# Weighing the values of four heads in one item, in the causal stage of a four-stage kernel

## The chip, the core and the metric

The kernel runs on one core of a Trainium2 chip. The metric is the device time of one execution in microseconds (us). Engines: PE (TensorE, matrix products into PSUM), DVE (VectorE), ACT (ScalarE), POOL (GpSimd), SP (which issues the DMAs here).

## The reference, cut to what matters

Four layers follow each other on x of shape (4, 1024, 128): attention over a window of 64, a gated linear attention, a causal attention mixed with a fast-weight recurrence, and a mixture of experts. The change is in the third:

```python
q, k, v = split(layernorm(x) @ Wqkv_w + Wqkv_b)        # 16 heads of 8 columns
scores = einsum('bhid,bhjd->bhij', q, k) * scale
attn = softmax(scores + causal_mask)                   # 1024 x 1024 per head, masked above the diagonal
y_softmax = einsum('bhij,bhjd->bhid', attn, v)
# y_stp: y_t = (W_static + state_t) q_t, state_t = retention * state + Gamma * v_t k_t^T
y = alpha * y_softmax + (1 - alpha) * y_stp            # alpha: a gate, per token and head
x = x + y @ out_w + out_b
```

## The kernel before, in words

The four stages run one after the other: window, gla, causal, moe. In the trace the causal stage's first scores are at 1058 us and its last weighing ends at 1750.

In the causal stage a unit is a batch b and a group g of four heads; there are 16. Queries are rows in chunks of 512 columns (c = 0, 1), keys are in blocks of 128 rows (j). A key step is a pair (c, j) that the mask doesn't empty: 4 for c = 0 and 8 for c = 1, 12 per unit. Its queries are those of chunk c from block j on. In a unit that is six steps of 512 columns, two of 384, two of 256 and two of 128.

PE works through one list of items, `order`, in that order, and the other engines go through the same list for their part of each item:

- M (lines 1092 to 1112): scores with queries on the partitions, for the row maxima. DVE reduces them (line 1261). 20 per unit, each of up to 2 x 512 columns. They belong to the unit after the one whose W and V surround them.
- S (1113): the negative maxima turned, after POOL has split them in three (1513 to 1519); ACT copies them (1365) and SP's DMAs put them into the stack as three more rows.
- W (1120 to 1138): scores with keys on the partitions, two heads (half i of the group) on two halves of the array's rows, bf16, then on a diagonal block two mask products (1133, 1136). ACT takes the exponential (1375) into one of four buffers `c_probs`.
- V (1139 to 1158): the weighing. For each of two heads an fp32 product of 128 key rows by 9 columns (8 values and a one, whose sum is the softmax's denominator) into partitions 32h of the accumulator `acc`, summed over j.
- A (1376): ACT copies a finished chunk's accumulator to `c_o_T`.

Beside them run the next batch's norm and projections (turn, q, k, v, gate1, gate2, vT), the finish of the previous batch (att, tp), and the recurrence: for each of 8 columns a product on POOL (kv, 1526), a scan on DVE (1271), a scale on ACT (1388) and two passes on POOL (read, 1538 and 1541), two columns per unit.

M, S, W, att, tp and the projections take turns in three PSUM slots of two banks, `ring`. Before PE writes an item it waits until the item three places earlier in the ring has been read (`pe_wait_free`, 1010). V doesn't use the ring: it goes to `acc`, of which there are two, one per chunk in turn.

The list is made by `causal_order` (855). It holds prices of each item for PE, ACT and DVE (`TIMES`, `times`), keeps a clock for each, and puts row scores M ahead of a W or V as long as they are at least 9 and at most 19 key scores ahead of need; between these bounds it does so where the item would begin no later than the W or V and DVE isn't behind ACT (`put_ahead`, 960). Each W is followed by the V of three W before:

Of the kernel before, what the change touches and what calls it, by code (L numbers as in the profile page):

```python
# [13 lines left out]
P = 128  # L14
BANK = 512
EPS = 1e-5
HEADS, HD = 16, 8
GROUP = 4
GROUPS = HEADS // GROUP
# [97 lines left out]
def build(nc, x_in, packed, x_out, place, batches, T, known):  # L117
# [7 lines left out]
    with ctx:  # L125
# [36 lines left out]
        acc = [accs[:, i * BANK:(i + 1) * BANK] for i in range(2)]  # L162
# [692 lines left out]
        def causal_order():  # L855
# [55 lines left out]
            def times(item):  # L911
# [4 lines left out]
                if item[0] in "WV":  # L916
                    c, j = item[3:5]
                    a = max(c * BANK, j * P)
                    cols = (c + 1) * BANK - a
                    if item[0] == "V":  # L920
                        return 0.02 + 0.00103 * cols, (), 0
                    return 0.00077 * cols + (0.15 if a == j * P else 0), (("A", 0.17 + 0.00166 * cols),), 1
# [6 lines left out]
            def begin(item):  # L929
                t = clock["P"]  # L930
                if times(item)[2]:
                    t = max(t, free[0])
                return max(t, made[item[1:]]) if item[0] == "V" else t

# [35 lines left out]
            for u in units:  # L970
                for k, (c, j) in enumerate(KEY_STEPS):
                    for i in range(2):
# [3 lines left out]
                        while sums:  # L976
                            put(sums.pop())
                        late.append(("V", *u, c, j, i))
                        if len(late) > 3:
                            item = late.pop(0)  # L980
                            put_ahead(item)
                            put(item)
                            if item[4:] == ((item[3] + 1) * BANK // P - 1, 1):
                                sums.append(("A", *item[1:4]))
                    for item in side[(u[0] * GROUPS + u[1]) * len(KEY_STEPS) + k]:
# [4 lines left out]
        def causal():  # L990
# [49 lines left out]
            def pe_program():  # L1040
# [3 lines left out]
                for item in order:  # L1044
# [94 lines left out]
                    elif kind == "V":  # L1139
                        _, b, g, c, j, i = item  # L1140
                        a = first_query(c, j)
# [4 lines left out]
                        pe.wait_ge(c_cleared, ("ones", 1))  # L1146
                        if j == 0 and i == 0 and ci >= 2:
                            pe.wait_ge(c_copied, ci - 2)
                        pe.wait_ge(c_weights_made, ("W", *item[1:]))
                        weights = c_probs[w_index["W", b, g, c, j, i] % 4]  # L1150
                        for r in range(2):
                            h = 2 * i + r
                            mm = nc.tensor.matmul(  # L1153
                                acc[ci % 2][32 * h:32 * h + HD + 1, a - c * BANK:BANK],
                                c_values[b % 2][:, j, r * HEADS // 2 + 2 * g + i, :],
                                weights[:, r * BANK:r * BANK + (c + 1) * BANK - a],
                                start=j == 0, stop=j == (c + 1) * BANK // P - 1, skip_group_check=True)
                        mm.then_inc(c_weighed.up(item), 1)
# [26 lines left out]
            def dve_program():  # L1185
# [10 lines left out]
                for item in order:  # L1196
# [42 lines left out]
                    elif kind == "v":  # L1239
                        _, b, h = item  # L1240
                        dv.wait_ge(c_valued, (b, h))
                        if b >= 2:
                            dv.wait_ge(c_weighed, ("V", b - 2, GROUPS - 1, *KEY_STEPS[-1], 1))
                        nc.vector.tensor_tensor(
# [57 lines left out]
            def act_program():  # L1302
# [5 lines left out]
                for item in order:  # L1308
# [58 lines left out]
                    elif kind == "W":  # L1367
# [5 lines left out]
                        if wi >= 4:  # L1373
                            ac.wait_ge(c_weighed, ("V", *w_items[wi - 4][1:]))
                        nc.scalar.activation(view(c_probs[wi % 4]), view(ps), ACT.Exp).then_inc(c_weights_made.up(item), 1)  # L1375
                    elif kind == "A":
                        _, b, g, c = item
                        ac.wait_ge(c_weighed, ("V", b, g, c, (c + 1) * BANK // P - 1, 1))
                        if b:
# [1244 lines left out]
```

## Time and profile before

| | |
|---|---|
| Time, median of 3 runs | 2084.08 us (2080.84 to 2087.06) |
| The profiled execution | 2081.97 us, its span 2080.6 us |
| PE busy | 1812.6 us, 87% |
| DVE busy | 1295.3 us, 62% |
| ACT busy | 1134.7 us, 55% |
| POOL busy | 660.3 us, 32% |

Busy time is that of instructions; the end of a matmul is modelled and holds the time its last results need to leave the array, which overlaps the next item. A record of a matmul starts where its columns start to stream, so the time an item takes on PE is best read from its start to the start of the next. An fp32 matmul leaves two records, a bf16 one leaves one.

### The profile page before, as it was taken

The numbers are of one execution on the slowest core, as the hardware profiler recorded it, in microseconds if no ns is written. First come the engines' busy times: TensorE is split into PE (matmuls) and PEld (weight loads), VectorE is DVE, ScalarE is ACT, GpSimd is POOL, SyncE is SP. The second block draws the span as 40 slices with busy tenths as digits, with TensorE's granted clock in tenths as the row PEclk, the third lists the DMA queues.
The fourth block names the chain that finished last, engine by engine and source line by source line (L and its number), as shares of the span: only waits on it lengthen the run. The fifth ranks groups of instructions, "written<-read, shape, count | busy, mean of one in ns | idle before, by whom it ended". The sixth has DMA issues, their size and how long they took to land.

```text
span 2080.6 us, 45291 instructions
## 1 busy us (share of the span) xinstructions
PE 1812.6 (87%) x19452; PEld 1056.7 (51%) x19472; DVE 1295.3 (62%) x2096; ACT 1134.7 (55%) x1720; POOL 660.3 (32%) x468
## 2 busy tenths in 40 slices
PE   4688879999999999999658899799889988598799
PEld 2456646776677677677522324233333423355465
DVE  5566536666666666666566776586677663555544
ACT  2365647667666766766315676566566665222221
POOL 5220004342343434235504442544444344000000
PEclk8899969999999999999858999899999999799999
DMA  6754000000000000000161532252262220000000
GB/s 166 215 132 96 7 9 1 2 1 1 2 2 1 1 2 2 1 2 2 73 148 42 161 77 50 88 137 63 82 143 62 62 63 21 0 11 6 6 11 11
DMA packets 38361, 102.08 MB, mean 49 GB/s; under 512 B 3856, under 2 KB 12176, under 8 KB 34704
## 3 DMA queue, kind: packets, MB, share of 16 engines
q1 hardware_dynamic: 38160, 99.18, 18.5%
q8 instruction: 153, 2.51, 0.5%
q14 instruction: 48, 0.39, 0.1%
HBM read 66.93 MB, written 31.46 MB: 47 GB/s over the span
## 4 chain that ended last, share of the span: by engine, by line
PE 56%; DVE 20%; issue 8%; ACT 5%; POOL 4%; DMA 1%; POOLq 0%; DVEq 0%; SPq 0%; ACTq 0%
PE accs L1153 8%; DVE arena L1261 4%; PE ring L1870 3%; PE accs L1934 3%; PE ring L2364 3%; PE ring L2366 3%; PE accs L2333 3%; PE ring L1896 3%; PE ring L1129 2%; PE ring L1103 2%; DVE arena L1271 2%; PE ring L1864 2%; PE ring L1835 2%; DVE arena L2023 1%; DVE arena L2063 1%
## 5 line engine op out<-in xcount | busy, mean ns | idle before, releaser
L1261 DVE TENSOR_REDUCE arena<-ring 128x2 f32<-128x1024 f32 (+2 forms) x320 | 346.1, 1112 | 148.1 <-PE ring L1110 97.2
L1375 ACT ACTIVATE arena<-ring 128x1024 f32<-128x1024 f32 (+3 forms) x384 | 304.3, 808 | 174.4 <-PE ring L1136 139.0
L1153 PE MATMUL accs<-arena 128*9 128x512 f32 (+3 forms) x1536 | 322.2, 500 | 0.0
L1129 PE MATMUL ring<-arena 51*128 51x512 bf16 (+3 forms) x768 | 133.5, 342 | 26.7 <-DVE arena L1261 14.8
L1103 PE MATMUL ring<-arena 48*128 48x512 bf16 (+3 forms) x768 | 131.5, 353 | 22.7 <-DVE arena L1261 10.0
L2248 POOL TENSOR_TENSOR arena<-arena 128x1280 f32<-128x1280 f32 x28 | 65.3, 2332 | 265.2 <-PE accs L1934 234.6
L1129 PEld LDWEIGHTS ring<-arena 51*128 51x128 bf16 x768 | 37.9, 94 | 207.0 <-issue 82.9
L2240 POOL TENSOR_TENSOR arena<-arena 128x512 f32<-128x512 f32 x112 | 138.9, 1272 | 10.2 <-DVE arena L2044 10.2
L2232 POOL TENSOR_TENSOR arena<-arena 128x1024 f32<-128x1024 f32 x32 | 75.6, 2364 | 190.2 <-DVE arena L2063 190.2
L2443 DVE TENSOR_TENSOR arena<-arena,ring 128x512 f32<-128x512 f32 x80 | 55.0, 688 | 122.7 <-PE ring L2366 112.2
L2493 ACT ACTIVATE arena<-ring 128x512 f32<-128x512 f32 x80 | 47.8, 597 | 147.0 <-PE ring L2364 147.0
L1538 POOL TENSOR_TENSOR arena<-arena 128x1024 f32<-128x1024 f32 x28 | 65.9, 2352 | 190.5 <-ACT arena L1388 147.9
L294 PE MATMUL ring<-weights_constants,xn 128*128 128x128 f32 x124 | 35.4, 379 | 84.1 <-DVE xn L278 52.6
L1271 DVE TENSOR_TENSOR_SCAN arena<-arena 128x1024 f32<-128x1024 f32 x32 | 79.5, 2484 | 34.5 <-POOL arena L1526 34.5
L2333 PEld LDWEIGHTS accs<-weights_large,arena 128*128 128x128 f32 x640 | 85.1, 193 | 29.2 <-issue 26.3
L2063 DVE TENSOR_TENSOR arena<-ring,arena 128x1024 f32<-128x1024 f32 x32 | 39.2, 1225 | 85.9 <-PE ring L1896 85.9
L1896 PE MATMUL ring<-arena 64*128 64x128 f32 x1024 | 91.7, 285 | 0.2
L1896 PEld LDWEIGHTS ring<-arena 64*128 64x128 f32 x1024 | 79.2, 187 | 19.5 <-issue 12.9
L2159 ACT ACTIVATE arena<-ring 128x1024 f32<-128x1024 f32 x32 | 32.8, 1024 | 100.7 <-PE ring L1835 100.7
L1996 DVE SCALAR_TENSOR_TENSOR arena<-ring,arena 128x1024 f32<-128x1024 f32 x32 | 39.2, 1225 | 76.0 <-ACT arena L2163 76.0
L1103 PEld LDWEIGHTS ring<-arena 48*128 48x128 bf16 x768 | 38.3, 97 | 94.9 <-issue 34.8
L2333 PE MATMUL accs<-weights_large,arena 128*128 128x128 f32 x640 | 85.0, 276 | 1.5 <-DVE arena L2449 0.5
(334 smaller groups left out, 4365.5 us busy)
## 6 DMA issues: line engine op xcount, KB each, us to landing
arena<-whole_k SPq DMA_DIRECT2D x32, 512.0 KB, 4.6
arena<-whole_q SPq DMA_DIRECT2D x32, 512.0 KB, 6.2
arena<-a_scratch_q SPq DMA_DIRECT2D x16, 384.0 KB, 6.9
arena<-a_scratch_k SPq DMA_DIRECT2D x16, 384.0 KB, 8.3
arena<-c_scratch_q SPq DMA_DIRECT2D x16, 384.0 KB, 8.2
arena<-c_scratch_k SPq DMA_DIRECT2D x16, 384.0 KB, 10.1
a_scratch_k<-arena SPq DMA_DIRECT2D x8, 512.0 KB, 3.9
c_scratch_k<-arena SPq DMA_DIRECT2D x8, 512.0 KB, 5.2
```

The costliest lines, as they stand in the source:

```text
L1103: mm = nc.tensor.matmul(o[r], qs[half(r, SCORE), pair, n * P:(n + 1) * P], ks[half(r, SCORE), pair, a:c], start=True, stop=not diag)
L1129: mm = nc.tensor.matmul(ps[:, r * BANK:r * BANK + cols], ks[half(r, SHIFT), pair, j * P:(j + 1) * P], qs[half(r, SHIFT), pair, a:a + cols] ...
L1153: mm = nc.tensor.matmul(acc[ci % 2][32 * h:32 * h + HD + 1, a - c * BANK:BANK], c_values[b % 2][:, j, r * HEADS // 2 + 2 * g + i, :], weig ...
L1261: nc.vector.tensor_reduce(dst, src, AX.X, ALU.max, negate=True).then_inc(c_max_taken.up(item), 1)
L1271: nc.vector.tensor_tensor_scan(sk[:, :], c_retain[:, j:j + 1].to_broadcast([P, T]), sk[:, :], 0.0, ALU.mult, ALU.add).then_inc(c_state_mad ...
L1375: nc.scalar.activation(view(c_probs[wi % 4]), view(ps), ACT.Exp).then_inc(c_weights_made.up(item), 1)
L1538: nc.gpsimd.tensor_tensor(sq[:, :], sk[:, :], sq[:, :], ALU.mult).then_inc(c_y_step.up((b, j)), 1)
L1896: mm = nc.tensor.matmul(ps[:, r * BANK + p * P:r * BANK + (p + 1) * P], k_[t % 2][half(r), p * P:(p + 1) * P], q_[t % 2][half(r), p * P:(p ...
L2232: nc.gpsimd.tensor_tensor(masked[0][:, :], masked[0][:, :], masked[1][:, :], ALU.add).then_inc(gla_joined.up(t), 1)
L2240: nc.gpsimd.tensor_tensor(pair_cols(q2m[t % 2][:, r, :]), pair_cols(q2[t % 2][:, :]), hot_b[:, r * P:(r + 1) * P].unsqueeze(1).to_broadcas ...
L2248: nc.gpsimd.tensor_tensor(state_mid[:, :, :, :].rearrange("p a r d -> p (a r) d"), state[:, :, :, :].rearrange("p a r d -> p (a r) d"), fa ...
L2333: mm = nc.tensor.matmul(total[:, n * P:(n + 1) * P], hid[index[item] % 3][:, n * P:(n + 1) * P], w("d_down", f * P, (f + 1) * P), start=f ...
```

## The change

V becomes an item of a key step, not of a half step: it weighs all four heads of the group with four matmuls in a row, from two `c_probs` buffers, and raises its semaphore once. The order becomes W(k, 0), W(k, 1), V(k−1): the weighing of a step comes behind both scores of the next. It waits for the second exponential of its step. What waited for V(…, 1) now waits for V of the step, and the exponential of W number wi waits for the V of the step in which W number wi − 4 was. The planner prices a V at 0.00205 us per column (four heads) where it was 0.02 + 0.00103 per column (two heads), and has one place for row scores ahead of a V per step. The scores and their masks, 128 columns wide, are as they were.

```diff
                     if item[0] == "V":
-                        return 0.02 + 0.00103 * cols, (), 0
+                        return 0.00205 * cols, (), 0
...
-                return max(t, made[item[1:]]) if item[0] == "V" else t
+                return max(t, made[item[1:] + (1,)]) if item[0] == "V" else t
...
                         while sums:
                             put(sums.pop())
-                        late.append(("V", *u, c, j, i))
-                        if len(late) > 3:
-                            item = late.pop(0)
-                            put_ahead(item)
-                            put(item)
-                            if item[4:] == ((item[3] + 1) * BANK // P - 1, 1):
-                                sums.append(("A", *item[1:4]))
+
+                    late.append(("V", *u, c, j))
+                    if len(late) > 1:
+                        item = late.pop(0)
+                        put_ahead(item)
+                        put(item)
+                        if item[4] == (item[3] + 1) * BANK // P - 1:
+                            sums.append(("A", *item[1:4]))
...
-                        _, b, g, c, j, i = item
+                        _, b, g, c, j = item
...
-                        if j == 0 and i == 0 and ci >= 2:
+                        if j == 0 and ci >= 2:
                             pe.wait_ge(c_copied, ci - 2)
-                        pe.wait_ge(c_weights_made, ("W", *item[1:]))
-                        weights = c_probs[w_index["W", b, g, c, j, i] % 4]
-                        for r in range(2):
-                            h = 2 * i + r
-                            mm = nc.tensor.matmul(
...
+                        pe.wait_ge(c_weights_made, ("W", *item[1:], 1))
+                        for i in range(2):
+                            weights = c_probs[w_index["W", b, g, c, j, i] % 4]
+                            for r in range(2):
+                                h = 2 * i + r
+                                mm = nc.tensor.matmul(
+                                    acc[ci % 2][32 * h:32 * h + HD + 1, a - c * BANK:BANK],
+                                    c_values[b % 2][:, j, r * HEADS // 2 + 2 * g + i, :],
+                                    weights[:, r * BANK:r * BANK + (c + 1) * BANK - a],
+                                    start=j == 0, stop=j == (c + 1) * BANK // P - 1, skip_group_check=True)
                         mm.then_inc(c_weighed.up(item), 1)
...
                         if wi >= 4:
-                            ac.wait_ge(c_weighed, ("V", *w_items[wi - 4][1:]))
+                            ac.wait_ge(c_weighed, ("V", *w_items[wi - 4][1:5]))
```

## Rows read from the trace of the kernel before

**Rows 1.** The page, part 4: the chain that ended last, by engine.

```profile
PE 56%; DVE 20%; issue 8%; ACT 5%; POOL 4%; DMA 1%; POOLq 0%; DVEq 0%; SPq 0%; ACTq 0%
```

**Rows 2.** Stretches: length, busy us of PE, PEld, DVE, ACT, POOL; granted clock; DMA.

```profile
0.00:600.00 600.00, 498.60 (x8113) 351.17 (x8114) 362.66 (x690) 353.76 (x579) 178.27 (x152) 0.93 0.21 55
1060.00:1089.00 29.00, 17.66 (x146) 7.17 (x142) 25.73 (x27) 1.01 (x1) 3.32 (x5) 0.50 0.37 78
1089.00:1750.00 661.00, 604.29 (x5484) 213.72 (x5486) 441.63 (x468) 413.57 (x523) 287.78 (x196) 0.95 0.33 84
1192.00:1262.00 70.00, 67.23 (x668) 21.80 (x666) 54.65 (x47) 47.14 (x59) 32.02 (x22) 1.00 0.31 76
1306.00:1367.00 61.00, 50.89 (x414) 18.74 (x416) 39.25 (x37) 33.82 (x41) 29.03 (x20) 0.89 0.50 137
1437.00:1481.00 44.00, 40.48 (x374) 17.99 (x372) 27.16 (x52) 26.57 (x37) 17.39 (x15) 0.99 0.20 50
1688.00:1723.00 35.00, 31.66 (x264) 8.72 (x260) 15.79 (x13) 23.34 (x29) 16.58 (x11) 0.90 0.26 62
1723.00:1750.00 27.00, 26.54 (x220) 7.38 (x218) 5.41 (x2) 22.05 (x29) 14.71 (x8) 1.00 0.16 40
```

**Rows 3.** Groups by line and shape: line 1153, busy us and mean ns.

```profile
L1153 PE MATMUL accs<-arena 128*9 128x512 f32 x768 | 204.2, 610 | 0.0
...
L1153 PE MATMUL accs<-arena 128*9 128x384 f32 x256 | 52.5, 488 | 0.0
...
L1153 PE MATMUL accs<-arena 128*9 128x256 f32 x256 | 39.5, 392 | 0.0
...
L1153 PE MATMUL accs<-arena 128*9 128x128 f32 x256 | 26.3, 288 | 0.0
```

**Rows 4.** Order of time: start us, length us, engine, line, what, count.

```profile
1209.36 0.39 PE L1129 MATMUL ring<-arena 51*128 51x512 bf16 x2
...
1209.59 0.38 PE L1103 MATMUL ring<-arena 48*128 48x512 bf16 x2
1209.80 1.02 ACT L1375 ACTIVATE arena<-ring 128x1024 f32<-128x1024 f32 x1 [0.37 <-PE ring L1129]
...
1209.90 1.03 PE L1153 MATMUL accs<-arena 128*9 128x512 f32 x4
...
1210.87 0.39 PE L1129 MATMUL ring<-arena 51*128 51x512 bf16 x2
...
1211.19 1.03 PE L1153 MATMUL accs<-arena 128*9 128x512 f32 x4
...
1214.26 0.38 PE L1103 MATMUL ring<-arena 48*128 48x512 bf16 x2
...
1214.57 1.03 PE L1153 MATMUL accs<-arena 128*9 128x512 f32 x4
1214.68 1.23 DVE L1261 TENSOR_REDUCE arena<-ring 128x2 f32<-128x1024 f32 x1 [0.21 <-PE ring L1103]
```

**Rows 5.** Order of time, PE, end of the stage.

```profile
1748.62 0.82 PE L1153 MATMUL accs<-arena 128*9 128x384 f32 x4
...
1749.61 0.94 PE L1153 MATMUL accs<-arena 128*9 128x256 f32 x16
1750.49 0.33 PE L1164 MATMUL ring<-weights_constants,arena 128*128 128x128 f32 x1
```

**Rows 6.** Line 1153 alone in two stretches of 0.05 us (x: matmul records).

```profile
1748.60:1748.65 0.05, 0.04 (x2) 1.00 0.00 0
1749.60:1749.65 0.05, 0.04 (x4) 1.00 0.00 0
```

**Rows 7.** Groups of DVE, 1100 to 1750 us.

```profile
L1261 DVE TENSOR_REDUCE arena<-ring 128x2 f32<-128x1024 f32 x173 | 206.9, 1220 | 63.9 <-PE ring L1103 47.2 <-PE ring L1110 15.4
L1271 DVE TENSOR_TENSOR_SCAN arena<-arena 128x1024 f32<-128x1024 f32 x32 | 79.5, 2484 | 34.5 <-POOL arena L1526 34.5
```

**Rows 8.** Group of line 1117, the sum S, with PE's idle time before it.

```profile
L1117 PE MATMUL ring<-ident,arena 128*12 128x128 bf16 x128 | 10.6, 230 | 12.1 <-POOL arena L1519 7.8 <-ACT arena L1332 4.2
```

More of the change, by code:

```diff
@@ L1146, in pe_program @@
                         pe.wait_ge(c_cleared, ("ones", 1))
-                        if j == 0 and i == 0 and ci >= 2:
+                        if j == 0 and ci >= 2:
                             pe.wait_ge(c_copied, ci - 2)
-                        pe.wait_ge(c_weights_made, ("W", *item[1:]))
-                        weights = c_probs[w_index["W", b, g, c, j, i] % 4]
-                        for r in range(2):
-                            h = 2 * i + r
-                            mm = nc.tensor.matmul(
[L1154 to L1157, printed above, removed]
+                        pe.wait_ge(c_weights_made, ("W", *item[1:], 1))
[8 more added lines that the diff above has]
+                                    start=j == 0, stop=j == (c + 1) * BANK // P - 1, skip_group_check=True)
                         mm.then_inc(c_weighed.up(item), 1)
@@ L1242, in dve_program @@
                         if b >= 2:
-                            dv.wait_ge(c_weighed, ("V", b - 2, GROUPS - 1, *KEY_STEPS[-1], 1))
+                            dv.wait_ge(c_weighed, ("V", b - 2, GROUPS - 1, *KEY_STEPS[-1]))
                         nc.vector.tensor_tensor(
@@ L1377, in act_program @@
                         _, b, g, c = item
-                        ac.wait_ge(c_weighed, ("V", b, g, c, (c + 1) * BANK // P - 1, 1))
+                        ac.wait_ge(c_weighed, ("V", b, g, c, (c + 1) * BANK // P - 1))
                         if b:
```

## The prediction

> **What bounds the kernel now.** Read first the page's chain of waits [rows 1]: more than half of the span hangs on PE, and the reader should ask in which stage that is. The stretches of the causal stage [rows 2] answer it. The stage proper runs from 1089 to 1750 us: PE is busy 604.3 of 661 us (91%), DVE 441.6 (67%), ACT 413.6 (63%). In the quiet stretch 1192:1262 (two units of 12 key steps, with no projections) PE is busy 67.2 of 70 us. There PE sets the pace. In 1306:1367, where the next batch is projected, PE is busy only 50.9 of 61 us: the rest is waiting for other engines' links in a chain.
>
> Next, what PE does there. Line 1153, the weighing, has 1536 matmul records, two for each fp32 matmul, four for a V item [rows 3]: 204.2 + 52.5 + 39.5 + 26.3 = 322.5 us, over half of PE's time in the stage. In the order of time [rows 4], a V over 512 columns starts at 1209.90, the next W at 1210.87: 0.97 us on PE's path, since the last 0.06 of its 1.03 overlap. W to M takes 0.23 us, W to V 0.32, M to V 0.31: going over to the weighing costs about 0.09.
>
> **Part 1: four heads in one item.** Half i writes PSUM partitions 64i to 64i+31 and 64i+32 to 64i+63, so the four matmuls of a step lie in four different column strips. Do they stream together? Before, a W always parts the two halves, except at the very end, where four V items stand in a row. There 16 records over 256 and 128 columns take from 1749.61 to 1750.49 = 0.88 us [rows 5]. Inside 0.05 us four of them start, where a lone V starts two [rows 6]. Two at a time would be two V of 256 columns (39.5 / 64 − 0.07 = 0.55 each) and two of 128 (26.3 / 64 − 0.07 = 0.34): 1.78 us. Four at a time is 0.55 + 0.34 = 0.89. So four heads cost PE what two did: 0.97 us at 512 columns instead of 1.93.
>
> PE's path loses half of (322.5 − 384 × 0.07) = 148 us, and 192 of 384 crossings to the weighing at 0.09 = 17 us: 165 us of work. The same fp32 products are made, with the same weights and moving tiles; 384 increments of a semaphore become 192; no DMA moves, and nothing passes a wait of SP's or POOL's queue.
>
> **Part 2: the weighing stands behind both W of the next step.** V waits for the second exponential of its own step, two W back instead of three. With one M between them the ring's slot for the second W has already made PE wait for that exponential, so 0. ACT's exponential of W(k+1, 0) waits for V(k−1), which stands before it on PE: V is over 1.03 us after its start, the W is issued at 0.97 and read 0.44 later (1209.36 to 1209.80), so 0. Behind that wait on ACT stand the copies A and S and the scale; they wait no longer than before. A comes once per chunk as before. Cover gone, either wait would cost at most an exponential's 1.02 us; 0 to 0.4 us in few of 192 steps is what the rows allow, and I take 0.
>
> **Part 3: the planner.** Its price for weighing a full step goes from 2 × (0.02 + 0.00103 × 512) = 1.09 to 1.05 us, practically the same. It was 1.8 times too cheap for what it described and is now about right. Row scores keep their lead of 9 to 19 key scores; there are three places per step to put one instead of four, and two will often stand close together.
>
> **Where the 165 us go.** Four ring items per step (2 W, about 1.75 M or S) share three slots. A slot comes back after W's 0.44 + 1.02 + some 0.05 = 1.5 us, or after M's 0.42 + 1.23 + 0.05 = 1.7 (M at 1214.26, DVE from 1214.68). Now a full step is 2 × (0.23 + 0.31 + 0.97) = 3.02 us of pure PE, and slots are back in time since each V of 0.97 covers the return. After, PE would need 4 × 0.23 + 0.09 + 0.97 = 1.98. But the first ring item behind a V must be back before the fourth goes, and only then comes the next V: 1.5 to 1.7, + 0.31, + 0.97 = 2.78 to 2.98. DVE's two reductions are 2.46. A step with one M is bound by ACT's two exponentials, 2.04, plus hops: 2.1. With 0.75 of the steps of the first kind: 0.75 × 2.88 + 0.25 × 2.1 = 2.69, against 0.75 × 3.02 + 0.25 × 2.79 = 2.96 now. That is 0.27 us × 6 full steps = 1.6 us per unit. The 384-column steps drop from 2.7 to some 2.5; the two 256 and two 128 steps are held by DVE (2.46 for two reductions) and give 0 to 0.4 each. Sum: 1.6 + 0.4 + 0.8 = 2.8 us per unit at least, since these chains take the worst order each time. The upper side: the most loaded engine sets a quiet unit, DVE with 54.7 / 2 = 27.3 of 35 us, so 7.7 saved. I take 4, nearer to the chains, because three slots leave DVE no queue.
>
> By stretches [rows 2]: 7 quiet units × 4 = 28. Four units with the attention's finish (1437:1481: PE 40.5 of 44, DVE 27.2, ACT 26.6, few row scores), PE down to about 30: 5 each, bounds 2 and 10, = 20. Three units with the projections, 61 us, a third of PE's saving lost in waits that stay: 4 each = 12, bounds 0 and 10. 1688:1723 has few row scores; 2.57 us a step falls to ACT's 2.1: 6. The last, 1723:1750, is pure PE (26.5 of 27) and becomes ACT's, 22.1 busy: 4. Together 70. Against it: the sum S, for which PE waited 12.1 us [rows 8] on POOL and ACT, comes sooner, and the two scans per unit (2.48 us on DVE [rows 7]) have less cover: both lie inside "4, not 7.7". The clock takes 4 (below). Net 66: 2082 (this execution: span 2080.6, 1.4 around it) becomes 2016; the median shown, 2084, is 2 higher, and I forecast **2017 us**.
>
> The clock [rows 2]: in 1060:1089, where PE only feeds DVE's reductions (17.7 of 29 us busy), the granted clock is 0.50, the lower level, 1.2 GHz. In 0:600 PE is busy 83% and the clock 0.93; in 1192:1262 it is 1.00. After, PE would be busy some 75 to 80% in quiet units, in small pieces; by the rows 0:600 that costs a few hundredths, 4 us in my sum. The Trainium skill (TensorE: Matmul & The Clock Gate, "A second HAM failure mode: psum-queue depth-cycling") warns of just this shape, frequent short idles between groups that wait for PSUM, and of a clock that swings. By that rule the gain shrinks or turns; it is rival D. The trace speaks only half for it: 0:600 waits so too and stays high.
>
> **Rivals.** A (70%): the above, 1975 to 2055.
> B (12%): slots bind less than I say; the most loaded engine sets each unit. 7 × 7.7 + 4 × 10 + 3 × 9 + 8 + 4.5 = 133 saved: 1950. For it: DVE and ACT have a third of idle time. Against: the three slots.
> C (9%): the 1.3 us block of V starves DVE and ACT each step and what PE saves is all given back; 2075 to 2090. For it: 2.98 against 3.02 in the worst order. Against: steps without row scores must gain.
> D (6%), slower: with PE idle in small pieces the clock falls in the stage as in 1060:1089. At 1.2 GHz a full step is PE 4 × 0.45 + 0.1 + 1.93 = 3.8 us against 3.02. It eats the gain (0.3 a full step) from about a quarter of the stage at the low level; at half of it the time is 2110.
> E (3%), the change doesn't do what it says: four matmuls don't stream together. The Trainium skill (same page, "The mechanism") says that weights load beside running matmuls only where row groups differ, and these all use the same 128 rows. The four starts within 0.05 us speak against it. Then V is 1.93 in one block, only 17 us of crossings go, and the ring starves longer: 2095.
>
> **How the numbers follow.** The likeliest is A: 2017. The range 1960 to 2075 takes in half of B and the edge of C. Less than 0.3% (6 us, what a measurement of this kernel can tell from no change) is most of C; D, E and a little of C are slower: faster 0.86, same 0.07, slower 0.07.
>
> **What would show it.** Four records of line 1153's shape starting together, its busy sum near 165 us; PE's idle in 1192:1262's successor from 3 to over 12 us per pair of units, released by lines 1261 and 1375; DVE's share in quiet units from 78% to 85 or 90; 512-column steps at 2.6 to 2.9 us; the last unit near 23 us and set by ACT. Wrong if line 1153 keeps 322 us (E), if the granted clock of the stage falls below 0.88 (D), or if PE idle grows by as much as its work falls (C).

## The result, and the profile after

The changed kernel takes 2048.62 us (median of 6, 2044.53 to 2056.35), the kernel before 2083.48 (median of 6 in all): a ratio of 0.9835, 95% interval 0.9813 to 0.9857. It is faster by 35 us, 1.7%. The forecast was 2017 (1960 to 2075): the time lies in the range, the gain is about half of the 66 us that were forecast. The profiled execution is 2048.85 us, its span 2047.5.

The page: busy time by engine, and the chain that ended last by engine, against [rows 1].

```profile
PE 1710.9 (84%) x19472; PEld 1046.7 (51%) x19472; DVE 1288.2 (63%) x2096; ACT 1127.3 (55%) x1720; POOL 658.5 (32%) x468
...
PE 52%; DVE 24%; issue 7%; ACT 5%; POOL 4%; DMA 1%; POOLq 0%; DVEq 0%; SPq 0%
```

The stretches of the causal stage (length, busy us of PE, PEld, DVE, ACT and POOL, granted clock, DMA), against [rows 2]. The first is the stage, then two quiet units, a unit with projections, one with the attention's finish, another with projections, and the last two units.

```profile
1094.00:1717.00 623.00, 498.20 (x5478) 203.47 (x5478) 434.65 (x467) 405.45 (x523) 285.63 (x196) 0.88 0.35 88
1193.00:1256.00 63.00, 52.44 (x676) 20.74 (x673) 51.88 (x46) 46.41 (x60) 30.52 (x21) 0.96 0.37 87
1297.00:1363.00 66.00, 50.20 (x414) 19.58 (x412) 39.75 (x37) 33.47 (x40) 30.35 (x21) 0.73 0.49 132
1427.00:1469.00 42.00, 34.77 (x380) 17.43 (x376) 28.46 (x53) 26.11 (x38) 18.42 (x15) 0.90 0.21 52
1469.00:1531.00 62.00, 45.69 (x414) 18.65 (x414) 39.02 (x36) 33.50 (x41) 30.37 (x21) 0.80 0.49 135
1664.00:1692.00 28.00, 22.14 (x257) 7.39 (x256) 13.54 (x11) 21.93 (x30) 12.98 (x10) 0.85 0.30 77
1692.00:1717.00 25.00, 19.80 (x206) 5.79 (x204) 5.41 (x2) 21.10 (x29) 14.56 (x8) 0.86 0.18 43
```

The stage went from 661 us to 623. PE is busy 498.2 us in it, 105 less; it idles 125 us, 68 more. DVE and ACT have the work they had. The granted clock of the stage fell from 0.95 to 0.88: by the trace TensorE is at the lower level, 1.2 GHz, for 152 us of the stage, before for 63. In the projection units shown it is 0.73 and 0.80.

The weighing by shape (line 1155 is 1153 of before), against [rows 3], and the matmul records of that line in 0.05 us, against [rows 6]:

```profile
L1155 PE MATMUL accs<-arena 128*9 128x512 f32 x768 | 113.9, 669 | 2.2 <-ACT arena L1377 2.2
...
L1155 PE MATMUL accs<-arena 128*9 128x384 f32 x256 | 26.8, 491 | 0.6 <-ACT arena L1377 0.6
...
L1155 PE MATMUL accs<-arena 128*9 128x256 f32 x256 | 22.8, 433 | 0.0
...
L1155 PE MATMUL accs<-arena 128*9 128x128 f32 x256 | 14.8, 305 | 0.9 <-ACT arena L1377 0.9
```

```profile
1206.84:1206.89 0.05, 0.04 (x4) 1.00 0.00 0
```

The sum is 178.3 us, 144 less than the 322.5 of before, and in this V four records start within 0.05 us. The scores' matmuls, W and M on the page, before and then after:

```profile
L1129 PE MATMUL ring<-arena 51*128 51x512 bf16 (+3 forms) x768 | 133.5, 342 | 26.7 <-DVE arena L1261 14.8
L1103 PE MATMUL ring<-arena 48*128 48x512 bf16 (+3 forms) x768 | 131.5, 353 | 22.7 <-DVE arena L1261 10.0
```

```profile
L1130 PE MATMUL ring<-arena 51*128 51x512 bf16 (+3 forms) x768 | 133.5, 360 | 63.2 <-DVE arena L1263 48.8
L1104 PE MATMUL ring<-arena 48*128 48x512 bf16 (+3 forms) x768 | 140.0, 372 | 54.1 <-DVE arena L1263 14.7
```

Why is PE's busy time only 105 us lower, when the weighing's is 144 lower? All other matmuls of the stage together grew from 335 to 343 us. The rest is overlap: the weighing's records overlapped those of their neighbours for 53 us before and for 23 after, since there are half as many seams.

Three steps in the order of time, against [rows 4]:

```profile
1206.31 0.39 PE L1130 MATMUL ring<-arena 51*128 51x512 bf16 x2 [0.66 <-DVE arena L1263]
...
1206.54 0.38 PE L1104 MATMUL ring<-arena 48*128 48x512 bf16 x2
...
1206.85 1.04 PE L1155 MATMUL accs<-arena 128*9 128x512 f32 x8
...
1207.83 0.61 PE L1130 MATMUL ring<-arena 51*128 51x512 bf16 x4
...
1208.89 1.04 PE L1155 MATMUL accs<-arena 128*9 128x512 f32 x8
1209.00 1.22 DVE L1263 TENSOR_REDUCE arena<-ring 128x2 f32<-128x1024 f32 x1 [0.49 <-PE ring L1104]
...
1209.87 0.39 PE L1130 MATMUL ring<-arena 51*128 51x512 bf16 x2
...
1210.86 1.05 PE L1155 MATMUL accs<-arena 128*9 128x512 f32 x8
```

A V over 512 columns now holds eight records and lasts from 1206.85 to the next item at 1207.83: 0.98 us for four heads, where two heads took 0.97. Between the second V at 1208.89 and the third at 1210.86 there are 1.97 us, a whole step with one (short) row-score item, in place of the 2.79 that the prediction counts for such a step before. But ahead of the W at 1206.31 PE had been idle for 0.66 us, and in such waits the rest went. The waits of PE in the stage (who waited for whom, us in total, times, longest), before and then after:

```profile
PE ring L1129 <- DVE arena L1261: 14.3, 27, 1.3
PE ring L294 <- POOL xn L287: 13.4, 24, 1.7
...
PE ring L1103 <- DVE arena L1261: 3.7, 8, 0.7
...
PE ring L1103 <- ACT arena L1375: 3.6, 11, 0.7
```

```profile
PE ring L1130 <- DVE arena L1263: 48.1, 60, 3.4
PE ring L1104 <- ACT arena L1377: 13.1, 20, 2.4
PE ring L294 <- POOL xn L287: 12.0, 21, 2.3
...
PE ring L1104 <- DVE arena L1263: 7.4, 13, 0.8
...
PE ring L1130 <- ACT arena L1377: 4.8, 10, 1.9
...
PE accs L1155 <- ACT arena L1377: 2.7, 6, 0.8
```

Key scores waiting for a ring slot that DVE has not yet read grew from 14.3 to 48.1 us, from 27 waits to 60, the longest from 1.3 to 3.4. With the row scores' own waits for DVE (3.7 and 7.4) that is 18.0 us before and 55.5 after; waits for the exponential grew from 3.6 to 20.6. In the unit with projections from 1305.9 to 1366.7 before, and from 1297.4 to 1363.4 after, the first of these waits alone:

```profile
PE ring L1129 <- DVE arena L1261: 1.1, 1, 1.1
```

```profile
PE ring L1130 <- DVE arena L1263: 4.9, 5, 3.4
```

A full step of a quiet unit, in the order of time, shows how such a wait comes about:

```profile
1241.17 1.04 PE L1155 MATMUL accs<-arena 128*9 128x512 f32 x8
1242.15 0.39 PE L1104 MATMUL ring<-arena 48*128 48x512 bf16 x2
...
1242.58 3.48 DVE L1263 TENSOR_REDUCE arena<-ring 128x2 f32<-128x1024 f32 x3 [0.82 <-PE ring L1104]
...
1243.86 0.39 PE L1130 MATMUL ring<-arena 51*128 51x512 bf16 x2 [0.80 <-DVE arena L1263]
...
1244.67 1.05 PE L1155 MATMUL accs<-arena 128*9 128x512 f32 x8
```

The M right behind the block of V is written at 1242.15. DVE has read it 1.66 us later, and only then does the W that takes its slot go, at 1243.86. With the V's 0.98 us before it and 0.81 us of scores behind it the step takes 3.50 us. The 28 stretches in the quiet units from one 512-column V to the next last 2.80 us on average, from 1.81 to 4.53; nine of them take 1.97 to 2.04 us and nine 3.50 to 3.54.

A second kind of place, PE and DVE in the order of time:

```profile
1217.17 2.28 DVE L1273 TENSOR_TENSOR_SCAN arena<-arena 128x1024 f32<-128x1024 f32 x1
...
1218.42 0.39 PE L1104 MATMUL ring<-arena 48*128 48x512 bf16 x2
...
1219.37 2.06 DVE L1263 TENSOR_REDUCE arena<-ring 128x2 f32<-128x1024 f32 x2
...
1220.62 0.23 PE L1130 MATMUL ring<-arena 51*128 51x128 bf16 x2 [1.42 <-DVE arena L1263]
```

DVE scans from 1217.17 to 1219.45. The row scores of 1218.42 lie ready behind it, DVE reduces them from 1219.37 on, and the W at 1220.62, which needs their slot, has waited 1.42 us. From the records of all 32 scans: the 4.5 us after a scan's start, 144 us in all, hold 54 of the stage's 125 us of idle PE, and 22 of 57 before. So less than half of the added idle time, 32 of 68 us, lies there; of PE's waits for DVE's maxima it is again about half.

The stage by kind of unit (from the first exponential of a unit to that of the next):

| units | before | after | forecast change | measured change |
|---|---|---|---|---|
| 7 quiet | 246.9 | 224.1 | −28 | −22.7 |
| 4 with the finish (the first has none) | 168.3 | 157.9 | −20 | −10.4 |
| 3 with projections | 183.3 | 187.9 | −12 | +4.6 |
| 1 with few row scores | 34.9 | 28.0 | −6 | −6.9 |
| the last | 26.8 | 25.6 | −4 | −1.2 |

The stage's length changed by −36.7 us; it began 3.9 us later. In the traces of the experiments that leave DVE's maxima whole it begins anywhere from 1091 to 1105 us, and why wasn't looked into, so the stage's length says more than these 3.9 us. Each of these figures is from one trace: the three units with projections last 60.1, 66.0 and 61.9 us after the change.

### The profile page after: what moved, and what is told of

The parts are those of the page before. It is cut to its first block, busy times and chain, and to the rows that moved or that the text cites. A ratio compares the mean times of both kernels' runs of the same rounds, so it can differ in the third digit from the quotient of the medians.

```text
span 2047.5 us, 45122 instructions
## 1 busy us (share of the span) xinstructions
PE 1710.9 (84%) x19472; PEld 1046.7 (51%) x19472; DVE 1288.2 (63%) x2096; ACT 1127.3 (55%) x1720; POOL 658.5 (32%) x468
## 4 chain that ended last, share of the span: by engine, by line
PE 52%; DVE 24%; issue 7%; ACT 5%; POOL 4%; DMA 1%; POOLq 0%; DVEq 0%; SPq 0%
DVE arena L1263 7%; PE accs L1155 4%; PE ring L1872 3%; PE accs L1936 3%; PE ring L2366 3%; PE ring L2368 3%; PE accs L2335 3%; PE ring L1898 3%; DVE arena L1273 2%; PE ring L1104 2%; PE ring L1130 2%; PE ring L1837 2%; PE ring L1866 2%; DVE arena L2025 1%; DVE arena L2065 1%
## 5 line engine op out<-in xcount | busy, mean ns | idle before, releaser
L1377 ACT ACTIVATE arena<-ring 128x1024 f32<-128x1024 f32 (+3 forms) x384 | 297.8, 808 | 128.5 <-PE ring L1137 97.0
L1104 PE MATMUL ring<-arena 48*128 48x512 bf16 (+3 forms) x768 | 140.0, 372 | 54.1 <-DVE arena L1263 14.7
L1155 PE MATMUL accs<-arena 128*9 128x512 f32 (+3 forms) x1536 | 178.4, 539 | 3.7 <-ACT arena L1377 3.6
```

What stands on the lines that cost most here:

```text
L1104: mm = nc.tensor.matmul(o[r], qs[half(r, SCORE), pair, n * P:(n + 1) * P], ks[half(r, SCORE), pair, a:c], start=True, stop=not diag)
L1155: mm = nc.tensor.matmul(acc[ci % 2][32 * h:32 * h + HD + 1, a - c * BANK:BANK], c_values[b % 2][:, j, r * HEADS // 2 + 2 * g + i, :], weig ...
```

## The experiments

Ratios are to the kernel before, run on the same chip in the same rounds. In each diff the base is the changed kernel unless it is said otherwise. Two theories stood against each other for the missing half. Ring: the three PSUM slots come back too late behind a block of V. Clock: PE idles in small pieces, its clock falls, and its own work gets slower where it is late.

How the stage's length changed by kind of unit, in us, one trace each. The first two columns part the change in grouping alone (e3_strips against the kernel before) and streaming (the changed kernel against e3_strips); the others are told below:

| units | grouping | streaming | e5 against changed | e6 against before | e12 against changed |
|---|---|---|---|---|---|
| 7 quiet | +14.0 | −36.7 | −14.8 | −9.1 | −6.2 |
| 4 with the finish | +6.0 | −16.4 | −6.8 | −7.6 | +0.8 |
| 3 with projections | +26.2 | −21.6 | −21.7 | −13.0 | −7.1 |
| 1 with few row scores | −2.1 | −4.9 | −1.9 | −3.7 | +3.8 |
| the last | −0.4 | −0.7 | −0.8 | 0.0 | +0.7 |
| the stage | +43.7 | −80.4 | −46.0 | −33.3 | −8.0 |

**e3_strips: grouping without streaming together.**

```diff
-                                h = 2 * i + r
+                                h = r
...
-                                    start=j == 0, stop=j == (c + 1) * BANK // P - 1, skip_group_check=True)
+                                    start=j == 0 and i == 0, stop=j == (c + 1) * BANK // P - 1, skip_group_check=True)
...
-                    nc.vector.memset(acc[i][:, :], 0.0).then_inc(c_sums_cleared.up("all"), 1)
+                    nc.vector.memset(acc[i][:, :], 1.0).then_inc(c_sums_cleared.up("all"), 1)
```

> The changed kernel with both halves of a step writing the column strips 0 and 1 (the weighed values of the second half are added to those of the first; strips 2 and 3 stay at one), so that two matmuls stream together and not four. Order, items and waits are as changed. It parts the change in two: grouping and order alone, against the streaming together. My account: V over 512 columns is 1.85 to 1.93 us in one block, PE's path is that of before less 17 us of crossings, and the ring starves behind a block twice as long: 2085 to 2125. Rival: the block does no harm and only the crossings count: 2060 to 2072.

2127.56 us (ratio 1.0209, 1.0179 to 1.0238), a little above the range. Its 512-column weighings and its stage:

```profile
L1155 PE MATMUL accs<-arena 128*9 128x512 f32 x768 | 201.3, 649 | 2.1 <-ACT arena L1377 2.1
```

```profile
1092.50:1796.30 703.80, 598.19 (x5478) 232.49 (x5478) 438.67 (x467) 406.02 (x523) 285.57 (x196) 0.93 0.31 78
```

The stage is 703.8 us, where the kernel before has 660.2 from exponential to exponential with the same weighing two at a time. So putting the weighing of a whole step, 1.9 us in one block, behind both W costs 43 us, and the streaming of four heads gives back 79 (2127.6 to 2048.6). The forecast's part 1 was right, and larger than the net shows. Of its part 2, too, the zeros hold: in the changed kernel PE's line 1155 waited 3.7 us on ACT in all, and no wait of the exponential is put down to line 1155. What costs is the block: PE's waits for DVE's maxima are 44 us in e3_strips, against 18 before. How much of the 43 the changed kernel's shorter block of 0.98 us still costs, this run doesn't say. By kind of unit 26 of the 43 us fall on the three units with projections.

**e4_between: V between the two W.**

```diff
                         while sums:
                             put(sums.pop())
-
+                        if i == 0 and late:
+                            item = late.pop(0)
+                            put_ahead(item)
+                            put(item)
+                            if item[4] == (item[3] + 1) * BANK // P - 1:
+                                sums.append(("A", *item[1:4]))
                     late.append(("V", *u, c, j))
-                    if len(late) > 1:
-                        item = late.pop(0)
-                        put_ahead(item)
-                        put(item)
-                        if item[4] == (item[3] + 1) * BANK // P - 1:
-                            sums.append(("A", *item[1:4]))
```

> The changed kernel with V(k-1) between W(k, 0) and W(k, 1) in place of behind both. It asks whether the place of the 1 us block matters. Ring theory: as many ring items per step, and the block still holds back one ring item of the three; but W(k, 1) now goes behind the block and its exponential comes later beside W(k+1, 0)'s, ACT's two exponentials are spread as the reductions are: a few us either way, 2035 to 2060. If the order behind both W was itself what costs, it gives 15 us or more: 2020 to 2035. V now waits for an exponential issued one W back; if that binds, 2060 or more, and line 1155's V shows idle time released by ACT's line 1377.

2070.82 us (0.9934, 0.9910 to 0.9957): 22 us slower than the changed kernel. The last of the three cases came true, with its sign (V is line 1154 here, the exponential 1376; the longest such wait in the changed kernel is 0.8 us, 2.7 in all):

```profile
PE accs L1154 <- ACT arena L1376: 22.3, 39, 1.8
```

Behind both W is the better place for an undivided V.

**e5_after_short_max and e6_before_short_max: DVE's row maxima halved, in both kernels.**

```diff
+                        keep = width // 2
...
+                            src = src[:, :, :, 0:keep]
+                        else:
+                            src = src[:, :, 0:keep]
```

> The changed kernel with DVE's row maxima taken over the first half of each piece's columns only (the rest of the maximum is left out): 1.23 us becomes some 0.7. Everything else, PE's work too, stays. Ring theory (slots come back too late, DVE's reductions above all, PE idle before lines 1104 and 1130 released by DVE's 1263): the time falls by 25 to 60 us below the changed kernel, to 1990 to 2025. Rival (clock): PE's own slow stretches carry the time, DVE's only a part: a fall of under 10 us.

> The same halved row maxima in the kernel before. Ring theory: there PE sets the pace and slots are back in time, so the fall is small beside that of e5_after_short_max: 5 to 20 us, to 2065 to 2080, from the steps of 128 and 256 columns. Rival: DVE was as much of a bound before as after: the same fall as in e5_after_short_max.

After: 1991.83 us (0.9555, 0.9532 to 0.9579), 57 below the changed kernel. Before: 2038.84 (0.9778, 0.9759 to 0.9797), 46 below. The stage of each, first exponential to last:

```profile
1079.50:1657.10 577.60, 478.36 (x5478) 199.53 (x5472) 307.34 (x465) 399.55 (x523) 290.76 (x196) 0.91 0.38 96
```

```profile
1078.80:1705.80 627.00, 589.71 (x5480) 210.74 (x5476) 302.81 (x465) 412.79 (x523) 292.92 (x196) 0.97 0.35 89
```

The stage lost 46 us after (623.5 to 577.6) and 33 before (660.2 to 627.0); the rest was saved before it, where row scores alone run. So DVE carries more of the time after the change, by 13 us, as the ring theory asks. But the second expectation failed: the kernel before hung on DVE as well, for 33 us of a stage that I had called PE's. In both kernels the units with projections gain most for their number (21.7 us in three after, 13.0 before). With the maxima halved in the changed kernel, what PE waits for most is the exponential: its line 1104 31.8 us, 69 times.

**e11_short_exp: ACT's exponential halved.**

```diff
-                        view = lambda ap: ap[:, :].rearrange("p (r c) -> p r c", r=2)[:, :, 0:cols]
+                        view = lambda ap: ap[:, :].rearrange("p (r c) -> p r c", r=2)[:, :, 0:cols // 2]
...
-                                    weights[:, r * BANK:r * BANK + (c + 1) * BANK - a],
+                                    weights[:, r * BANK:r * BANK + ((c + 1) * BANK - a) // 2].unsqueeze(1).to_broadcast([P, 2, ((c + 1) * BANK - a) // 2]),
```

> The changed kernel with ACT's exponential over the first half of each score's columns only; the weighing reads that half twice (the second half's weights are left out). PE's work stays; an exponential of 1.02 us becomes 0.6. In the quiet units halved maxima gave 1.7 us of 32 each, though DVE had been busy 26 of them: so W's slot should bind there. Ring theory: a slot of W comes back after 1.1 us instead of 1.5, 0.4 us less per full step and some in the others: quiet units from 32 to 28 to 30 us, 2015 to 2035 in all. Rival (DVE and its scans bind, not ACT): quiet units stay at 31 to 32, 2040 to 2050.

2035.56 us (0.9753, 0.9730 to 0.9776), 13 below the changed kernel. The stage:

```profile
1096.00:1709.50 613.50, 490.35 (x5478) 201.00 (x5478) 432.97 (x467) 290.23 (x523) 285.55 (x196) 0.88 0.35 90
```

PE idles 613.5 less its busy time, 123 us, as in the changed kernel (125); the quiet units stay at 31 to 35 us (224.9 in all, 224.1 in the changed kernel), the last falls from 25.6 to 23.7, the three with projections from 187.9 to 182.0. W's slot, 1.5 us in my chain, is not what the quiet units wait for. That arm of the ring theory fell; DVE's arm stands.

**e7_half_columns, e9_half_from_second, e12_half_start_once: a shorter block.** Four heads by half of a step's columns, one such item behind each W. The planner's price of such an item is 0.1 us and 0.00168 per column, and it has four places per step for row scores again. The last pair of lines is e12_half_start_once's; in the other two both halves keep `start=j == 0`.

```diff
+                        a, z = (a0, a0 + cut) if part == 0 else (a0 + cut, (c + 1) * BANK)
...
-                                    acc[ci % 2][32 * h:32 * h + HD + 1, a - c * BANK:BANK],
+                                    acc[ci % 2][32 * h:32 * h + HD + 1, a - c * BANK:z - c * BANK],
...
-                                    start=j == 0, stop=j == (c + 1) * BANK // P - 1, skip_group_check=True)
+                                    start=j == 0 and part == 0, stop=j == (c + 1) * BANK // P - 1, skip_group_check=True)
```

> The changed kernel with the weighing of a step in two items of four heads and half the columns each (256 of 512; 256 and 128 of 384; 128 and 128; 128 whole): one behind each W of the next step. Four strips still stream together, the block is 0.54 us and not 0.97, and PE pays 12 more crossings per unit at 0.09 us, 17 us in all. Ring theory: the block that stands between a slot's return and the next ring item is halved; a full step is W to the M that takes its slot, 1.5 us, less the two gaps, 2 x 1.27 = 2.5 us against 2.8 to 3.0: 2015 to 2035, below the changed kernel by 15 to 35. Rival (PE's work or its clock counts): 17 us more work gives 2050 to 2065.

2038.90 us (0.9789, 0.9766 to 0.9811). In it the second half's start flag undoes the first half's accumulation of step 0, which it so leaves out.

> As e7_half_columns, but the first step of each chunk (j = 0), which starts the accumulation, is weighed in one item over all its 512 columns; halves only from j = 1 on. e7_half_columns measured 2038.9 us, 10 below the changed kernel, where the ring theory asked 15 to 35 (DVE's halved maxima were worth 57). If the time with halves comes from the shorter block, 2 of 6 full steps go back to the long one: 2038 to 2045. Rival: the halves gained only by chance of the clock's low stretches: 2044 to 2055, the same as the changed kernel.

2042.97 us (0.9796, 0.9767 to 0.9825), five runs from 2034.84 to 2053.19. The interval overlaps both the changed kernel's and that of e7_half_columns, so the time alone decides nothing; the stage in its trace is 618.1 us, between the 623.5 of the changed kernel and the 615.3 of e7_half_columns, as the shorter block asks.

> e7_half_columns with the accumulation's start flag raised only by the first half of a chunk's first step; the second half writes columns whose written marks that start has just cleared in its bank and strip, and so overwrites. All steps but those of 128 columns are in halves. Expected: the time of e7_half_columns, 2034 to 2044, 6 to 14 us under the changed kernel, with the reference's output. If the gain of halves was a matter of the clock's low stretches, 2044 to 2055.

2038.77 us (0.9776, 0.9749 to 0.9804). Its stage:

```profile
1093.90:1709.50 615.60, 521.64 (x6758) 225.14 (x6758) 441.98 (x467) 411.45 (x523) 286.19 (x196) 0.88 0.35 90
```

PE idles 94 us where the changed kernel idles 125, and is busy 23 us more, where I had counted 17 for the added crossings. Cutting the block is worth 10 us, twice measured, below the 15 to 35 I expected. That it is the block's length and not the fourth place for row scores wasn't tried apart. Of the kernels here that leave nothing out it is the fastest.

**e1_fill_v, e2_fill_turn, e10_fill_waits: keeping PE busy.** Matmuls with weights of zeros: in each V, over its columns (e1); in each V and, with 512 columns, ahead of the waits for normalised tiles (e2); or, with 512 columns, only ahead of such long waits (e10). The first addition below is that of e1 and e2, the second that of e2 and e10, ahead of the wait.

```diff
+                        mm = nc.tensor.matmul(acc[ci % 2][0:64, a - c * BANK:BANK], w3["half_rows"][:, 64:128],
+                                              w3["moe_bcast"][:, 0:(c + 1) * BANK - a],
+                                              start=False, stop=True, skip_group_check=True)
...
+                        nc.tensor.matmul(ps[0:64, BANK:2 * BANK], w3["half_rows"][:, 64:128], w3["moe_bcast"][:, 0:BANK],
+                                         start=True, stop=True, skip_group_check=True)
```

> The changed kernel with one more matmul at the end of each V: bf16, 64 columns of zeros as weights, as many moving columns as the step has, added into the same accumulator (it adds zero). It costs PE some 0.2 to 0.3 us per key step, 40 to 55 us of work. Two theories for why 165 us less PE work gave only 35 us: (clock) PE idles in small pieces, the granted clock of the causal stage fell from 0.95 to 0.88, and PE's own work got slower where it is late; (ring) three PSUM slots, each held 1.5 to 1.7 us, set the pace and the clock costs little. Clock: the added work fills idle time, the stage's granted clock comes back to 0.93 or more, and the time falls by 8 to 25 us below the changed kernel, to 2025 to 2040. Ring: the filler stands in front of the next ring item in most steps, the clock rises or not, and the time grows by 15 to 45 us, to 2065 to 2095.

2070.69 us (0.9937, 0.9908 to 0.9965; ten runs from 2060.95 to 2083.72), stage clock 0.90. PE is busy 42 us more in the stage; half of that filled idle time (125 to 104.6 us), and the stage grew by the other half.

> As e1_fill_v, and in the causal stage's eight transposes per batch of the normalised tiles three more zero-weight bf16 matmuls of 512 columns ahead of each wait for the tile (into the unused half of the item's own slot), where PE waits for POOL anyway. It asks whether the units with the next batch's projections (59 to 66 us, which got longer by 0 to 5 us instead of shorter by 4) lose to the clock: its mean there is 0.73 to 0.84. Clock theory: these three units come back to 55 to 59 us each, in all 5 to 15 us less than e1_fill_v. Ring or chain theory: the same as e1_fill_v within 3 us, since what they wait for is a chain of other engines.

2076.32 us (0.9951, 0.9928 to 0.9974), stage clock 0.93, units with projections 61.2 us on average (64.8 in e1's profile): better than e1 there by 11 us in all, but not the 55 to 59 expected, and the other units gave it back.

> The changed kernel with zero-weight bf16 matmuls of 512 columns only where PE waits for long anyway in the causal stage: eight before the first tile of each four normalised tiles to be turned, two before each other one, three before the sum S; none in V. In the changed kernel the granted clock was low for 20 us at 1290 and at 1461 and 17 at 1126, in those waits. Clock theory (of the 35 to 66 us that are missing, some 10 to 20 are lost there): stage clock from 0.88 to 0.92 or more, units with projections from 62.6 us on average to 58 to 60, 2036 to 2044. Rival: the clock's low stretches lie where PE waits on others' chains and cost nothing on the path: 2046 to 2055.

2058.37 us (0.9866, 0.9844 to 0.9888), 10 above the changed kernel. The stage:

```profile
1097.00:1722.80 625.80, 517.24 (x5607) 210.36 (x5607) 434.11 (x467) 406.46 (x523) 285.90 (x196) 0.92 0.35 88
```

The clock came back from 0.88 to 0.92 and the three projection units went from 62.6 us on average to 59.0, 11 us in all; the fillers cost as much elsewhere (three of the four units with the finish rose by 2.5 to 3.2 us, and the quiet ones by 4.6 in all). That the 11 us are the price of the low clock is argued, not shown: without filler the same three units sum to 175.8 us in e9_half_from_second and to 184.0 in e8_true_prices, where the changed kernel's trace has 187.9 and this one 177.1, so part of it may be chance.

**e8_true_prices: the planner's prices of scores taken from the trace.**

```diff
-                    mask = 0.15 * per if c == (n + 1) * P else 0
-                    return 0.00077 * per * (c - a) + mask, (("D", 0.16 + 0.00204 * per * (c - a)),), 1
+                    mask = 0.09 * per if c == (n + 1) * P else 0
+                    return 0.01 + 0.00043 * per * (c - a) + mask, (("D", 0.16 + 0.00204 * per * (c - a)),), 1
...
-                    return 0.00077 * cols + (0.15 if a == j * P else 0), (("A", 0.17 + 0.00166 * cols),), 1
+                    return 0.01 + 0.00043 * cols + (0.09 if a == j * P else 0), (("A", 0.17 + 0.00166 * cols),), 1
```

> The changed kernel with the planner's PE prices of scores as the trace has them: 0.01 + 0.00043 us per column and 0.09 for the mask, in place of 0.00077 per column and 0.15. Only the places of the row scores change. It asks whether the order of M is where the gain went. If it was: 10 us or more below the changed kernel, 2015 to 2038. If the three slots bind in any order: within 8 us, 2041 to 2057.

2051.58 us (0.9837, 0.9811 to 0.9863): no difference from the changed kernel that these runs can tell. This one other order of the row scores brings nothing; its quiet units take 235.1 us against 224.1, so the order does matter unit by unit, and an order that spreads the row scores evenly over the steps wasn't tried.

## Why the prediction was half right, point by point

The time fell in the range and the direction was right. The gain was 35 us and not 66, and the clock's fall was foreseen as a rival, not in the sum.

- **Part 1, four strips stream together: right.** Four records within 0.05 us, a V of four heads at 0.98 us, the line's sum 178.3 us where about 165 was named. 17 of the 96 weighings over 512 columns last up to 1.90 us in place of 1.05, all of them at the lower level of the clock for some or all of their time, and that makes 13 us of the sum. Rival E is refuted, and the rule on row groups that it quoted doesn't hold here, since all four strips use the same 128 rows; e3_strips shows what it would have cost, 2128, not my 2095.
- **Part 2, the new waits: right.** Line 1155 waited 3.7 us in all, the exponential never for V.
- **The chain of slots: the right mechanism, and one link of it.** The prediction put the price of the block there, 2.78 to 2.98 us per full step, with W's slot (1.5) or M's (1.7). e11_short_exp shows that W's slot doesn't bind in the quiet units. M's does: 0.98 + 1.71 + 0.81 = 3.50 us in the step shown above, since masks and a third M stand in the last link, where I had 0.31. A step with one row score takes about 2.0 us, below my 2.1. The average, 2.80, lies in the 2.6 to 2.9 that were named. The scans add to it; they were in the text, but "inside 4, not 7.7".
- **Quiet units: −22.7 against −28, and the unit with few row scores −6.9 against −6: the right size.** DVE is busy 51.9 of 63 us, 82%, where I expected 85 to 90. PE's idle time in the pair of units went from 3 to 10.6 us, not to over 12.
- **Units with the finish: −10.4 against −20.** The term was mis-sized. PE idles 7.2 of 42 us in the unit shown, with DVE at 28.5 and ACT at 26.1: nobody is full. In all four PE's waits for the exponential and for DVE's maxima grew most.
- **Units with projections: +4.6 against −12. This is the term that failed.** I took part of PE's saving for granted. PE's work there fell by 14 us in the three units, where an even share of the 165 is 31, and its idle time rose by 18. Most of the new waits are for DVE's maxima, 5.4 us before and 18.1 after in the three, while the links through POOL's tiles and ACT's parts that I had seen there hardly moved (16.6 and 18.0). Grouping alone made these units 26 us longer and streaming took only 22 back; halving the maxima takes 22 off them. So by these runs the block of V and DVE's maxima cost time there as elsewhere, and more. In one such unit the clock fell to 0.73, and e10_fill_waits, which fills the waits, has 11 us less in the three, with the doubt given there.
- **The clock: 4 us in the sum, 0.95 to 0.88 in the trace.** It made the weighing's records longer by 13 us in all, and all other matmuls grew by 8 (335 to 343 us). Not all of it lies on the path, and fillers that lifted the clock never paid. Rival D's condition was met: 0.88 between the two levels means 24% of the stage at the lower one, the "about a quarter" at which D saw the gain eaten, and D's sign, a clock below 0.88, is just reached (0.878). But 35 us of gain stayed, so its price was too high. The Trainium skill (TensorE: Matmul & The Clock Gate, "A second HAM failure mode: psum-queue depth-cycling") tells of a clock that swings when PE idles often and briefly, and the trace agrees in kind, with 63 us at the lower level before and 152 after. In [rows 2] I had read 0.93 at 83% busy as nearly harmless.
- **"PE sets the pace": too simple.** e6_before_short_max takes 33 us out of that stage with PE's work as it was.
- **Slips of the arithmetic.** 2084 less 66 is 2018, not 2017. Rivals D and E hold 9% and are both slower, where the last line gives slower 7%.

What stays open: of the 68 us of added idle PE, some 38 are waits for DVE's maxima and 17 for the exponential by the trace, and how they split between long maxima, scans and the order of items isn't known. The 54 us after scans are counted from the records, not tried by moving a scan; no run took the scans away, and none gave the ring a fourth slot.

## What to carry to other kernels

When the busiest engine gets a large cut, price first what a longer undivided item does to the slots that others wait for, unit by unit: here the grouping cost 43 us, 26 of them in three units of sixteen, and the streaming brought 79. Then look at the next engine's instructions that the old slack had hidden: a maximum of 1.22 us that returns the slot, a scan of 2.3 us before it. A busiest engine isn't yet the bound: halving DVE's maxima took 46 us off the kernel in which PE was busy 91% of the stage. If an item must be grouped to fill an array, try to cut it along another axis: four heads by half the columns kept the streaming and gave 10 us more.

## What the runs showed of the hardware

- Four fp32 matmuls of 128 rows by 9 columns in four column strips, each with its own 512 moving columns from the same 128 partitions, take 0.98 us to the next item at a granted clock of 1; two take 0.97.
- With a start flag on both halves of a bank's columns the sums lack what the first half held (e7_half_columns). With one flag, on the first half alone, and nothing else different, they are whole (e12_half_start_once): one flag covers all 512 columns of the strip.
- Matmuls with weights of zeros raise the granted clock too: it is 0.90 in all three units with projections of e10_fill_waits, where the changed kernel has 0.84, 0.73 and 0.80.
